# Weight-magnitude sums of a quantised feed-forward layer: spread over the tiles of the output projection, on two queues

## The reference, cut to what matters

```python
def _quant_weight(w):
    scale = jnp.mean(jnp.abs(w)) + EPS
    wq = jnp.clip(jnp.round(w / scale), -1.0, 1.0)
    return (wq, scale)

def _qlinear(x, w):
    wq, ws = _quant_weight(w)
    xq, xs = _quant_act(x)
    y = jnp.einsum('bsi,oi->bso', xq, wq)
    return y * xs * ws

gate = jax.nn.silu(_qlinear(x, w_gate))
up = _qlinear(x, w_up)
return _qlinear(gate * up, w_down)
# x = x + attention(xn) + ffn(xn)
```

## Time and profile before

| | us |
|---|---|
| median of the 2 runs | 10705.64 (10686.85 to 10724.42) |
| the profiled execution | 10580.49 |
| its span, slowest core | 10578.9 |
| spans of the 8 cores | 10496.2 to 10578.9 |
| TensorE busy | 6330.7 (60%) |
| DVE busy | 3050.3 (29%) |
| ACT busy | 2180.9 (21%) |
| GpSimd busy | 1166.6 (11%) |

### The profile page before, as it was taken

The page is one execution under the profiler, slowest core; times in us unless marked ns, Lnnn a source line. Parts: engine busy times, 40 slices in busy tenths (PEclk is TensorE's granted clock), DMA queues, the critical chain, the costliest instruction groups (busy, mean ns, idle before and its releaser), DMA issues.

```text
span 10578.9 us, 80970 instructions; the slowest of 8 cores (10496.2 to 10578.9 us)
## 1 busy us (share of the span) xinstructions
PE 6330.7 (60%) x26738; PEld 2863.2 (27%) x26738; DVE 3050.3 (29%) x4411; ACT 2180.9 (21%) x3834; POOL 1166.6 (11%) x1481
## 2 busy tenths in 40 slices
PE   0127666766766666659950008999999044427548
PEld 0112232323323322324420003444444022203213
DVE  4862232132122212320112223333332166600000
ACT  0000242034104401430002222222222311131220
POOL 0000000000000000000001114333332300031220
PEclk9758767866776677669975559999999566668779
DMA  8542001200210021023346663333332244448558
GB/s 263 138 114 62 25 4 51 65 9 8 69 47 4 8 78 38 8 68 84 82 133 235 234 236 113 111 114 113 112 112 80 95 123 129 123 108 161 124 131 152
DMA packets 1131870, 1048.14 MB, mean 99 GB/s; under 512 B 798786, under 2 KB 922307, under 8 KB 1088195
## 3 DMA queue, kind: packets, MB, share of 16 engines
q1 hardware_dynamic: 873412, 497.58, 18.7%
q10 hardware_dynamic: 230400, 344.04, 10.6%
q0 software_dynamic: 27648, 201.34, 5.2%
HBM read 824.68 MB, written 218.10 MB: 99 GB/s over the span
## 4 chain that ended last, share of the span: by engine, by line
PE 53%; DMA 19%; DVE 12%; ACT 5%; issue 4%; DVEq 3%; ACTq 2%; SPq 1%; POOLq 1%; POOL 0%
PE p L1268 8%; PE p L1270 8%; DMA wdp<-wdT 7%; PE p L1518 6%; DVE pt_l L713 2%; PE p L1008 2%; PE p L1010 2%; PE p L1009 2%; DMA zqf<-zq_sp 2%; PE p1qA L785 2%; DMA wsb<-wuT 2%; DMA wsb<-wdT 2%; PE p1qA L786 2%; PE p1qA L787 2%; DMA wsb<-wgT 2%
## 5 line engine op out<-in xcount | busy, mean ns | idle before, releaser
L1268 PE MATMUL p<-wgq,xqf 128*128 128x512 bf16 x4096 | 1555.7, 380 | 113.7 <-POOL dum L1159 113.7
L1270 PE MATMUL p<-wuq,xqf 128*128 128x512 bf16 x4096 | 1555.6, 380 | 0.0
L1518 PE MATMUL p<-wdq,zqf 128*128 128x512 bf16 x4096 | 972.2, 401 | 604.8 <-POOL dum L1436 546.4
L1518 PEld LDWEIGHTS p<-wdq,zqf 128*128 128x128 bf16 x4096 | 411.4, 102 | 1162.0 <-issue 735.5
L979 POOL DMA_DIRECT2D wsb<-wgT x64 | 33.9, 530 | 4950.6 <-DVE dum L748 3977.6
L1268 PEld LDWEIGHTS p<-wgq,xqf 128*128 128x128 bf16 x4096 | 401.4, 98 | 604.2 <-issue 124.5
L1270 PEld LDWEIGHTS p<-wuq,xqf 128*128 128x128 bf16 x4096 | 401.4, 98 | 483.4 <-issue 3.5
L1433 POOL TENSOR_TENSOR wdq<-sd 128x512 bf16<-128x512 f32 x256 | 322.7, 1261 | 1868.2 <-ACT sd L1399 1868.1
L1504 PE MATMUL p3t<-idb_t,zqp 128*128 128x128 bf16 x1024 | 119.4, 309 | 683.2 <-DVE zqp L1463 366.1
L785 PE MATMUL p1qA<-xnh_s,wp_h 128*128 128x512 bf16 x1024 | 401.9, 392 | 190.0 <-issue 83.0
L1246 PE MATMUL p<-ws 128*3 128x1 f32 x2 | 0.2, 163 | 854.2 <-DVE dum L1170 854.2
(11 more groups left out here) (221 smaller groups left out, 10036.8 us busy)
## 6 DMA issues: line engine op xcount, KB each, us to landing
zqf<-zq_sp SPq DMA_DIRECT2D x48, 2048.0 KB, 13.0
wsb<-wgT POOLq DMA_DIRECT2D x64, 1024.0 KB, 6.1
wsb<-wuT POOLq DMA_DIRECT2D x64, 1024.0 KB, 6.2
wsb<-wdT POOLq DMA_DIRECT2D x64, 1024.0 KB, 6.3
wgp<-wgT ACTq DMA_DIRECT2D x256, 256.0 KB, 2.7
wup<-wuT ACTq DMA_DIRECT2D x256, 256.0 KB, 3.0
z_sp<-zt SPq DMA_DIRECT2D x256, 256.0 KB, 2.0
zp<-z_sp SPq DMA_DIRECT2D x64, 1024.0 KB, 7.0
```

The source lines that it names most:

```text
L1268: eng.matmul(pg[:], lt, wgq[ib % 2][:, ec * 512:(ec + 1) * 512], start=(ec == 0), stop=(ec == 15))
L1270: ii = eng.matmul(pu[:], lt, wuq[ib % 2][:, ec * 512:(ec + 1) * 512], start=(ec == 0), stop=(ec == 15))
L1518: ii = eng.matmul(p3[idx % 2][:], lt, wdq[:, ic * 512:(ic + 1) * 512], start=(ic == 0), stop=(ic == 63))
```

## The change

GpSimd loads only DVE's blocks, into the first buffer, each behind the wait for DVE's previous one. The loads of ACT's blocks move to SP, with a semaphore of their own (`qY`), into the second buffer. SP issues 6 of them in every tile, behind x and y_sp, and all but the very first wait for ACT's previous block (`s1z`). DVE's reductions move into its loop over the tiles, 6 behind the two adds of each tile. With `TCN` = 16 tiles and 96 blocks on either side both slices `nsj * tch // TCN` to `nsj * (tch + 1) // TCN` are 6 long.

```diff
-    qZ = c.DQ("qZ", 2)
+    qZ = c.DQ("qZ", 1)
+    qY = c.DQ("qY", 1)
@@ SP, at the end of each tile's orders
+            nsjs = len(SJS)
+            for k in range(nsjs * tch // TCN, nsjs * (tch + 1) // TCN):
+                j = SJS[k]
+                (wd_, r0, c0, w, col) = SJ[j]
+                if k >= 1:
+                    eng.wait_ge(s1z, k)
+                mk[("z", j)] = qY.inc(eng.dma_start(
+                    out=wsb[1][:, 0:w], in_=wd_[r0:r0 + 128, c0:c0 + w]), 0)
@@ GpSimd
-        for j, (wd_, r0, c0, w, col) in enumerate(SJ):
-            if j >= 2:
-                pj = j - 2
-                if pj % 2 == 0:
-                    eng.wait_ge(v1z, pj // 2 + 1)
-                else:
-                    eng.wait_ge(s1z, pj // 2 + 1)
-            mk[("z", j)] = qZ.inc(eng.dma_start(out=wsb[j % 2][:, 0:w],
+        for k, j in enumerate(SJV):
+            (wd_, r0, c0, w, col) = SJ[j]
+            if k >= 1:
+                eng.wait_ge(v1z, k)
+            mk[("z", j)] = qZ.inc(eng.dma_start(out=wsb[0][:, 0:w],
                                                 in_=wd_[r0:r0 + 128, c0:c0 + w]),
-                                  j % 2)
+                                  0)
@@ DVE, inside the loop over the tiles instead of behind it
-        for j in SJV:
-            (wd_, r0, c0, w, col) = SJ[j]
-            qZ.wait(eng, mk[("z", j)])
-            eng.tensor_reduce(out=c.wsum[:, col:col + 1], in_=wsb[j % 2][:, 0:w],
-                              axis=AX, op=OP.add,
-                              apply_absolute_value=True).then_inc(v1z, 1)
+            nsjv = len(SJV)
+            for k in range(nsjv * tch // TCN, nsjv * (tch + 1) // TCN):
+                j = SJV[k]
+                (wd_, r0, c0, w, col) = SJ[j]
+                qZ.wait(eng, mk[("z", j)])
+                eng.tensor_reduce(out=c.wsum[:, col:col + 1], in_=wsb[0][:, 0:w],
+                                  axis=AX, op=OP.add,
+                                  apply_absolute_value=True).then_inc(v1z, 1)
@@ ACT
-            qZ.wait(eng, mk[("z", j)])
-            eng.activation(out=wsb[j % 2][:, 0:w], in_=wsb[j % 2][:, 0:w],
+            qY.wait(eng, mk[("z", j)])
+            eng.activation(out=wsb[1][:, 0:w], in_=wsb[1][:, 0:w],
                            func=AF.Abs, bias=0.0, scale=1.0,
                            accum_out=c.wsum[:, col:col + 1]).then_inc(s1z, 1)
```

## The result

| | us |
|---|---|
| before, median of 10 runs | 10705.64 (10576.53 to 10863.22) |
| changed, median of 11 runs | 10160.34 (10098.31 to 10351.84) |
| ratio | 0.954, 95% interval 0.9482 to 0.9597 |
| the profiled execution | 10180.3 (span 10178.8, core 5) |
| forecast | 10219, range 10070 to 10440 |

Some executions of either kernel had cores at a lowered granted clock; the ratios leave them out, while medians with their spreads take in all executions.

The account below looks back on a forecast made before the run. The round trip of load, reduction and next load bounds the stage's end; after the change, SP's orders pace the tiles. 28.6 + 34 + 0.4 gives P = 63, and 9336.7 + 14 P gives 10219 us, range 10070 to 10440.

Parts of the forecast that it names:

- The tail: End of the output projection without matmuls: 853.7 us, 95 pairs of wsb loads, 9.0 us a pair, set by round trips.
- DMA's work: Transfers in one tile: twelve loads at 2.9 us plus 11.6 us of the tile's own traffic, 46 us a tile.
- P: Pace of one output projection tile with 12 loads inside it; forecast 63 us.
- SP's chain: SP's line of orders in each tile, expected to set the pace: 28.6 + 34 + 0.4 = 63 us.
- T: Time at which SP issues oh for a tile; SP's first wsb load was forecast at T + 9.
- DVE's chain: Six rounds a tile of GpSimd's order, load and DVE's reduction, 8.9 us each: 53.4 us.
- what TensorE sees: Per tile: ol lands at about T + 14, matmuls take 43.4 us, adds 5, TensorE idles some 20 us.
- rival A: In the tiles, DVE's chain or TensorE's loop paces: P 54, time 10093 us; chance 0.13.
- rival C: No faster: TensorE's clock stays low in the tiles, P 92, time 10664 us; chance 0.05.
- The ends: Before and after the tiles: T(1) at 4821.5, 108.5 us from T(15) to the end, stage end 4930 + 14 P.
- B: DMA engines get crowded in the tiles, landings 8.4 us: P 81, time 10471 us; chance 0.18.
- D: All loads but the last six hidden under 41.4 us tiles: 808 us less, time 9898 us; chance 0.02.

Follow-up runs that it names:

- third profile: The changed kernel again, nothing altered, as control in a later session: median 10177.74 us, ratio 0.9507 to the kernel before; its profile has the stage at 1106 us.

## Why the prediction was right, and where it was not

**The mechanism and its size.** The tail was a row of round trips, and they went under the matmuls. The stage lost 492 us on the mean of the cores, 487 were forecast. That the two agree to 5 us is partly luck: the sum was made from core 7, and that core lost 520 (below). The means of the profiled spans differ by 424 (10550.5 to 10126.5), which is the 492 less the 75 of the down product, with 4 and 3 from attention and gate and up. The medians differ by 545; by stages that can't be laid open, as only profiled executions have them.

**DMA's work.** 46 us a tile and 0.73 at P = 63 were forecast; 0.75 at 61 measured, 46 us. The 46 us held as long as two loads were in flight, and not in the run with four.

**SP's chain, P = 63.** It measured 60.5 on core 5 and 61.3 on the mean, and the working held in its parts, on the cores where this chain paces. One tile of it in the timelines of ACT and SP, core 5:

```profile
5106.24 1.91 ACT L1054 ACTIVATE wsb<-wsb 128x2048 f32<-128x2048 f32 x1 [6.05 <-DMA wsb<-wuT]
...
5116.50 1.91 ACT L1054 ACTIVATE wsb<-wsb 128x2048 f32<-128x2048 f32 x1 [8.26 <-DMA wsb<-wuT]
...
5137.73 1.91 ACT L1054 ACTIVATE wsb<-wsb 128x2048 f32<-128x2048 f32 x1 [19.23 <-DMA wsb<-wuT]
...
5146.60 1.91 ACT L1054 ACTIVATE wsb<-wsb 128x2048 f32<-128x2048 f32 x1 [6.86 <-DMA wsb<-wuT]
...
5153.52 1.91 ACT L1054 ACTIVATE wsb<-wsb 128x2048 f32<-128x2048 f32 x1 [4.92 <-DMA wsb<-wuT]
```
```profile
5108.73 0.38 SPq L952 DMA_DIRECT2D osb_h<-oh_sp  x1
5109.16 7.01 SPq L954 DMA_DIRECT2D osb_l<-ol_sp  x1
5116.26 5.09 SPq L958 DMA_DIRECT2D xb<-x  x1
5121.44 0.38 SPq L963 DMA_DIRECT2D y_sp<-ty  x1
5121.92 34.01 SPq L971 DMA_DIRECT2D wsb<-wuT  x4
```

T is 5108.73. ol holds the queue for 7.0 us (7.9 forecast), and x, which I had at 0.3, for 5.1, so z0 goes out at T + 13.2 and not T + 9. ACT starts on it at T + 29.0. This tile is longer than most: over 15 tiles of the core z0 goes out at T + 10.9, and ACT starts on it at T + 26.1, where 26.4 was forecast. Its start on z0 comes 19.4 us behind that on z5, and the five other rounds take 8.4 each (8.5 forecast): 19.4 + 5 x 8.4 = 61. The third profile's 63.1 is no better hit of 63: its cores ran at a lowered clock.

**DVE's chain, 53.4: the step that failed.** "Already this is more than TensorE's 41.4 us", it said, and left it 10 us below SP's. Its rounds on core 5, from one reduction to the next, means over 15 tiles, the first one across the adds: 10.2, 12.5, 10.9, 9.3, 8.6, 8.4. The sum is 60.0, not 6 x 8.9. The last three are near the 8.9 of the tail. The first three fly beside oh, ol, x and y_sp. The sum had charged that burst to SP's chain (7.2 us for GpSimd's loads in it) and not to DVE's, though they fly at the same time. The paragraph on what TensorE sees even has "53 us and some 6 more in the burst", so 59; neither the bound of 53.4 nor rival A was brought up to it. The same sentence said that late reductions would matter only two tiles on. They matter at once, as SP's x waits for the adds behind them: on core 7 in every tile. The rounds in DVE's timeline, one tile, core 5:

```profile
5094.25 2.29 DVE L1041 TENSOR_REDUCE wsum<-wsb 128x1 f32<-128x2048 f32 x1 [5.72 <-DMA wsb<-wgT]
5102.31 2.29 DVE L1041 TENSOR_REDUCE wsum<-wsb 128x1 f32<-128x2048 f32 x1 [5.78 <-DMA wsb<-wgT]
5106.25 2.29 DVE L1032 TENSOR_TENSOR ty<-p,bo_b 128x2048 f32<-128x2048 f32 x1 [1.65 <-PE p L1016]
...
5111.62 2.29 DVE L1041 TENSOR_REDUCE wsum<-wsb 128x1 f32<-128x2048 f32 x1 [0.72 <-DMA wsb<-wgT]
5121.67 2.29 DVE L1041 TENSOR_REDUCE wsum<-wsb 128x1 f32<-128x2048 f32 x1 [7.76 <-DMA wsb<-wgT]
5136.82 2.29 DVE L1041 TENSOR_REDUCE wsum<-wsb 128x1 f32<-128x2048 f32 x1 [12.86 <-DMA wsb<-wuT]
5147.22 2.29 DVE L1041 TENSOR_REDUCE wsum<-wsb 128x1 f32<-128x2048 f32 x1 [8.12 <-DMA wsb<-wuT]
5157.29 2.29 DVE L1041 TENSOR_REDUCE wsum<-wsb 128x1 f32<-128x2048 f32 x1 [7.78 <-DMA wsb<-wuT]
```

From 5111.62 they follow each other by 10.1, 15.2, 10.4, 10.1; before the burst by 8.0. The error did no harm to the time, as SP's chain was as long, which was luck. It did to the reading: rival A (DVE paces, P 54) was a case I gave 0.13 as a faster kernel, and DVE's chain does pace on core 7 and where ACT issues its own, but at 61. That is also why the moved orders on SP are worth nothing: I had their cost right and took it for the bound.

**TensorE.** 43.4 us for a tile and 20 of idle were forecast, 60.5 - 16.8 = 43.7 and 16.8 measured. The clock came back in every tile (rival C fell): the granted clock is 0.87 over the stretch, and late in each tile the matmuls start 0.216 us apart. It costs 2.3 us a tile against 41.4, and nothing on the path.

**The ends.** Behind the last tile 51.3 us were forecast, 5 for the adds, 45.8 for six reductions and 0.5. DVE's last first add starts at 5717.1, the next stage's first instruction at 5768.8: 51.7. On core 7, from whose profile the sum was made, the stage fell from 1589 to 1069, by 520. There P is 61.1, not 63, which is 26 us of the 33 that this is above the forecast.

**The rivals.** B needed P of 69 and rounds over 10 us; the largest P of a core in any profile of the changed kernel was 63.6. Its mechanism is there, but small: landings went from the tail's 6.2 to 6.5 and 6.8, where B had 8.4. D needed rounds of 6.9: not seen with two chains. It came true only when half of the loads were gone from the stage.

**One load by itself.** With one chain alone the landings are 5.0 to 5.2 and P is 54.5 and 54.8; with both, 6.5 to 6.8 and 61. The Trainium skill, "DMA: Bandwidth & Descriptors" (anatomy of one DMA, which the page has for GpSimd's path), gave a load of 1 MB at 4.4 us, and with it P 54 as an estimate. The landings of a chain by itself are 0.6 to 0.8 us above the page's figure, and those of this kernel 2.1 to 2.4. That P 54 lies by the 54.5 and 54.8 of the single chains is chance, as the estimate was for both chains together. With SP, ACT or GpSimd as the issuer P is 59.8 to 61.3, which agrees with the same page's "Issuing engines are not separate DMA queues": a second issuer saves only the time of issuing.

## What to carry to other kernels

When serial round trips move under other work, write down every chain that shares the DMA engines, and charge each one with the bursts of the others; then the second-longest chain tells what relieving the longest can bring, here 2 us of 61. A tail that goes one load at a time is better cut in number than in pace: more in flight went from 61 to 55, half the loads went to the matmuls' own 41.4, though 178 to 226 of the 304 to 334 us came back in the stage that took the other half. When a chain is run alone, look at what the critical chain then goes through: ACT's alone read 54.8, and much of its path was TensorE's. Compare stages, not totals, when a stage behind the change spreads by more than the effect: 491 and 492 us in the stage stood beside 424 and 482 in the mean spans. And look at the clock of the stage as well: the third profile had 462.

## What the runs showed of the hardware that I had not expected

A 1 MB load from HBM lands in 5.0 to 5.2 us beside the traffic of one tile, in 6.5 to 6.8 with a second such stream, and the streams differ by side: read from SBUF, both together are at 4.8 to 5.6.

The time that the DMA engines are busy for the same bytes isn't constant: 47 us a tile at a share of 0.77 with loads of 1 MB, 52 at 0.93 with loads of 512 KB. No stretch of 400 us or more read here moved over 291 GB/s on a core, at shares up to 0.94.

The granted clock has a third value under matmuls without a pause, and it comes and goes on some cores alone. It came in the output projection too, with the longer tiles of the third profile and of the run with ACT's blocks only. In the run with half in attention, two stretches of the gate and up product on core 6; column before the last two is the clock:

```profile
6200.00:6250.00 50.00, 49.44 (x190) 20.33 (x188) 14.86 (x30) 12.13 (x18) 16.30 (x18) 0.81 0.28 91
6800.00:6850.00 50.00, 50.00 (x234) 22.67 (x232) 17.71 (x36) 14.84 (x22) 20.33 (x23) 1.00 0.33 111
```

TensorE is as busy in both, and makes 190 matmuls at 0.81 where it makes 234 at 1.00. The stage took 2084 us on core 6, and 1894 on core 4, whose clock was 1.00. Of the pairs 0 and 1, 2 and 3, 4 and 5, 6 and 7 both cores went alike, each time that this occurred. The Trainium skill, "TensorE: Matmul & The Clock Gate", Part 1, has a limiter that takes a die to 13/16 (0.81) once three of its cores run dense matmuls, for as long as they do. The value agrees with the row. Two other points don't. It doesn't hold while the load lasts, as the second row shows, and it doesn't take a whole die: from 6000 to 6800 us of this run the clock is 0.86 on cores 6 and 7 beside 1.00 on 4 and 5, and all eight cores run the same matmuls. The page has the limit depend on the data, and the weights of this stage are -1, 0 and 1. But in the output projection of the kernel before, with the bf16 parts of Wo, all eight cores were at 1.00 from 4800 to 5400 us.
